# Two 3x3 convolutions read three horizontally shifted copies of their input instead of windows of one padded copy

## The reference, cut to what matters

```python
x_top    = conv1x1(x, w_top);  x_center = conv1x1(x, w_center)     # 16 channels each
x_bottom = conv3x3(x, w_bottom, pad=1)                             # 128 channels
sp_map = einsum('bnp,bpm->bnm', x_center, x_top)                   # 256 x 256 per image
sp_map = softmax(sp_map.reshape(bsz, -1), axis=1)                  # one softmax per image
sp_map = einsum('bnm,bmc->bnc', sp_map, x_bottom)
return conv3x3(x + sp_map.reshape(x.shape), w_out, pad=1)
```

## Time and profile before

| | |
|---|---|
| median of 3 runs | 411.04 us (409.38 to 413.88) |
| the profiled execution | 410.04 us, of which the span in the trace is 408.3 us |
| first convolution, start of its first and last matmul | 14.59 and 31.50 us of the span |
| second convolution, the same | 31.75 and 49.70 us |
| PE busy | 386.3 us, 95% of the span |
| DVE, ACT, POOL busy | 258.3, 282.5, 152.6 us |

### The profile page before, as it was taken

The page is one execution under the profiler, slowest core; times in us unless marked ns, Lnnn a source line. Parts: engine busy times, 40 slices in busy tenths (PEclk is TensorE's granted clock), DMA queues, the critical chain, the costliest instruction groups (busy, mean ns, idle before and its releaser), DMA issues.

```text
span 408.3 us, 5044 instructions
## 1 busy us (share of the span) xinstructions
PE 386.3 (95%) x1641; PEld 273.7 (67%) x1641; DVE 258.3 (63%) x557; ACT 282.5 (69%) x502; POOL 152.6 (37%) x126
## 2 busy tenths in 40 slices
PE   8999989989999889999999999999999999988993
PEld 3588656443646667787787767877777777655782
DVE  0654246884342688566774995766957497777774
ACT  4241235945210967777979989999999998887881
POOL 3810000740085427421458584121232366332253
PEclk9999999999999999999999999999999999999998
DMA  8940000000000023571111004034040002120331
GB/s 263 451 165 0 2 1 0 1 2 0 0 2 0 1 64 109 219 284 53 26 32 46 0 8 125 28 80 177 3 129 26 27 26 79 52 79 0 104 101 56
DMA packets 10674, 28.77 MB, mean 70 GB/s; under 512 B 1079, under 2 KB 2231, under 8 KB 10392
## 3 DMA queue, kind: packets, MB, share of 16 engines
q1 hardware_dynamic: 10648, 28.45, 20.5%
HBM read 27.82 MB, written 0.62 MB: 70 GB/s over the span
## 4 chain that ended last, share of the span: by engine, by line
PE 64%; ACT 17%; DVE 15%; issue 3%; POOLq 0%; POOL 0%; ACTq 0%; DVEq 0%
PE ps L411 16%; PE ps L412 15%; PE ps L413 15%; ACT hidh L966 5%; ACT ps L967 4%; PE ps L418 3%; DVE hidl L1287 2%; PE ps L656 2%; PE ps L423 2%; ACT rstd L875 2%; ACT rstd L877 2%; PE ps L602 1%; DVE bot L1209 1%; DVE small L1208 1%; PE ps L646 1%
## 5 line engine op out<-in xcount | busy, mean ns | idle before, releaser
L1287 DVE TENSOR_TENSOR hidl<-ps,hidh 128x512 fp32r<-128x512 f32 x160 | 108.6, 687 | 52.7 <-ACT ps L967 51.1
L382 POOL TENSOR_TENSOR x<-x,parts 128x512 f32<-128x512 f32 x43 | 55.8, 1298 | 148.1 <-DVE parts L1297 99.7
L411 PE MATMUL ps<-xh,wh_all 128*128 128x512 f32 x160 | 73.0, 456 | 2.2 <-DVE hidl L1287 1.3
L966 ACT ACTIVATE hidh<-ps,par 128x512 fp32r<-128x512 f32 x96 | 68.1, 709 | 8.5 <-PE ps L413 6.8
L411 PE MATMUL ps<-hidh,wh_all 128*128 128x512 f32 (+1 forms) x162 | 64.3, 397 | 4.4 <-DVE hidl L1287 3.8
L967 ACT ACTIVATE ps<-ps,par 128x512 f32<-128x512 f32 x96 | 65.4, 681 | 0.0
L412 PE MATMUL ps<-hidh,wl_all 128*128 128x512 f32 (+1 forms) x162 | 63.5, 392 | 0.0
L412 PE MATMUL ps<-xh,wl_all 128*128 128x512 f32 x160 | 63.5, 397 | 0.0
L413 PE MATMUL ps<-hidl,wh_all 128*128 128x512 f32 (+1 forms) x162 | 63.3, 390 | 0.0
L413 PE MATMUL ps<-xl,wh_all 128*128 128x512 f32 x160 | 63.0, 393 | 0.0
L372 POOL TENSOR_TENSOR wl_all<-wa,wh_all 128x512 fp32r<-128x512 f32 x40 | 50.7, 1283 | 3.5
(11 more groups left out here) (227 smaller groups left out, 569.2 us busy)
## 6 DMA issues: line engine op xcount, KB each, us to landing
scores_all<-rows_scratch SPq DMA_DIRECT2D x48, 256.0 KB, 3.3
wa<-in_moe SPq DMA_DIRECT2D x2, 4096.0 KB, 16.5
wa<-in_moe SPq DMA_DIRECT2D x1, 2048.0 KB, 9.4
dft_x<-in_dft_x SPq DMA_DIRECT2D x1, 640.0 KB
dft_o<-in_dft_o SPq DMA_DIRECT2D x1, 640.0 KB
w<-in_w_bottom SPq DMA_DIRECT2D x1, 576.0 KB, 7.0
w<-in_w_out SPq DMA_DIRECT2D x1, 576.0 KB, 8.8
cst<-in_consts SPq DMA_DIRECT2D x1, 512.5 KB, 7.8
```

The lines of the kernel that those rows point to most:

```text
L382: pool.tensor_tensor(half(x, h), half(x, h), parts[:, n % 2, :], ALU.add).then_inc(s["state_added"], 1)
L411: pe.matmul(o, wh, xhi, start=start, stop=False)
L966: act.activation(hidh[:, n % 2, f, :], sums, func, bias=bias).then_inc(s["hidden_hi_act"], 1)
L1287: dve.tensor_tensor(hidl[:, n % 2, f, :], bank(sums_bank(n, f)), f32(hidh[:, n % 2, f, :]), ALU.subtract).then_inc(s["hidden_lo"], 1)
```

## The change

`xph` and `xpl` are kept three times, once for each horizontal shift `dx`, as [3, 4 images, 18 rows, 16 pixels]: the rows keep their border above and below, and have none left and right, since copy `dx` holds the columns dx to dx+15 of `xp`. A window of a tap is then, per image, 16 rows that follow each other without a gap, 256 elements. The taps run by column: dx = 0 with its three dy first, then dx = 1, then dx = 2. PE waits ahead of each dx for that copy alone. `top` and `cen` move into `wb`, which is free at that time.

```diff
-            xph = sb("xph", [C, B, PAD, PAD], F32R, scope)
-            xpl = sb("xpl", [C, B, PAD, PAD], F32R, scope)
+            xph = sb("xph", [C, 3, B, PAD, SIDE], F32R, scope)
+            xpl = sb("xpl", [C, 3, B, PAD, SIDE], F32R, scope)
...
+        top, cen = wb[:, 0, 0:PIX], wb[:, 0, PIX:2 * PIX]
...
+        def shifted(t, h, dx):
+            return t[:, 2 * h:2 * h + 2, :, dx:dx + SIDE]
...
                 for h in halves:
-                    pe.wait_ge(hi_done, n0 + h + 1)
-                    pe.wait_ge(lo_done, n0 + h + 1)
                     for t in range(9):
                         if (h, t) in between:
                             between[h, t]()
-                        dy, dx = divmod(t, 3)
-                        wh = w33h[:, which, t * C:(t + 1) * C]
-                        wl = w33l[:, which, t * C:(t + 1) * C]
-                        win = (slice(None), slice(2 * h, 2 * h + 2), slice(dy, dy + SIDE), slice(dx, dx + SIDE))
+                        dx, dy = divmod(t, 3)
+                        if dy == 0:
+                            if dx < 2:
+                                pe.wait_ge(early_hi, 2 * h + dx + 1)
+                                pe.wait_ge(early_lo, 2 * h + dx + 1)
+                            else:
+                                pe.wait_ge(hi_done, n0 + h + 1)
+                                pe.wait_ge(lo_done, n0 + h + 1)
+                        w = (3 * dy + dx) * C
+                        wh = w33h[:, which, w:w + C]
+                        wl = w33l[:, which, w:w + C]
+                        win = (slice(None), dx, slice(2 * h, 2 * h + 2), slice(dy, dy + SIDE), slice(None))
...
+            def shift_high(h, dx):
+                act.wait_ge(s["normed"], h + 1)
+                ins = act.activation(xph[:, dx, 2 * h:2 * h + 2], shifted(xp, h, dx), ACT.Copy)
+                ins.then_inc(s["shift_hi" if dx < 2 else "norm_hi"], 1)
+
             for h in range(2):
-                act.wait_ge(s["normed"], h + 1)
-                act.activation(xph[:, 2 * h:2 * h + 2].rearrange("p b y x -> p (b y x)"),
-                               xp[:, 2 * h:2 * h + 2].rearrange("p b y x -> p (b y x)"), ACT.Copy).then_inc(s["norm_hi"], 1)
+                shift_high(0, h)
...
+            shift_high(0, 2)
+            for dx in range(3):
+                shift_high(1, dx)
```

On DVE the low parts of `xp` are six instructions instead of two (`norm_lo` is signalled by the third copy of each half), spread over the list; those of `yp` are six instead of two, in place:

```diff
-            for h in range(2):
-                dve.wait_ge(s["norm_hi"], h + 1)
+
+            def shift_low(h, dx):
                 dve.wait_ge(s["normed"], h + 1)
-                seg = [t[:, 2 * h:2 * h + 2].rearrange("p b y x -> p (b y x)") for t in (xpl, xp, xph)]
-                dve.tensor_tensor(seg[0], seg[1], f32(seg[2]), ALU.subtract).then_inc(s["norm_lo"], 1)
+                if dx < 2:
+                    dve.wait_ge(s["shift_hi"], 2 * h + dx + 1)
+                else:
+                    dve.wait_ge(s["norm_hi"], h + 1)
+                ins = dve.tensor_tensor(xpl[:, dx, 2 * h:2 * h + 2], shifted(xp, h, dx), f32(xph[:, dx, 2 * h:2 * h + 2]), ALU.subtract)
+                ins.then_inc(s["shift_lo" if dx < 2 else "norm_lo"], 1)
+
+            for dx in range(3):
+                shift_low(0, dx)
...
                 dve.tensor_reduce(mx[:, b:b + 1], bank(b), AX.X, ALU.max).then_inc(s["score_max"], 1)
+            shift_low(1, 0)
             dve.wait_ge(s["max_turned"], 1)
...
             dve.tensor_copy(nmx, bank(6, cols=B, first=256)).then_inc(s["neg_max"], 1)
+            shift_low(1, 1)
+            shift_low(1, 2)
             shift_weights(0)
             shift_weights(1)
```

More of the change, by code:

```diff
@@ L84 @@
     "borders_zero", "quiet_zero", "wb_split", "wo_split", "we_split", "pool_step",
-    "centered", "squared", "variance", "log_var", "rstd", "normed", "norm_hi", "norm_lo",
+    "shift_hi", "shift_lo", "mix_shift_hi", "mix_shift_lo", "centered", "squared", "variance", "log_var", "rstd", "normed", "norm_hi", "norm_lo",
     "dve_step",
@@ L142, in metaformer @@
             bot_t = sb("bot_t", [C, TT, C], scope=scope)
-            top = sb("top", [C, PIX], scope=scope)
-            cen = sb("cen", [C, PIX], scope=scope)
             we = sb("we", [C, E * C], scope=scope)
@@ L448, in _, with conv33 @@
                     last.then_inc(s["proj_done"], 1)
-            def conv33(which, hi, lo, hi_done, lo_done, n0, done, halves=(0, 1), between={}):
+            def conv33(which, hi, lo, early_hi, early_lo, hi_done, lo_done, n0, done, halves=(0, 1), between={}):
                 for h in halves:
-                    pe.wait_ge(hi_done, n0 + h + 1)
-                    pe.wait_ge(lo_done, n0 + h + 1)
                     for t in range(9):
@@ L511, in _ @@
             pe.wait_ge(s["wb_split"], 1)
-            conv33(0, xph, xpl, s["norm_hi"], s["norm_lo"], 0, s["bottom_done"],
+            conv33(0, xph, xpl, s["shift_hi"], s["shift_lo"], s["norm_hi"], s["norm_lo"], 0, s["bottom_done"],
                    between={(0, 6): turn_max, (0, 7): spread_max,
@@ L525, in _ @@
             pe.wait_ge(s["wo_split"], 1)
-            conv33(1, xph, xpl, s["mix_hi"], s["mix_lo"], 0, s["out_conv_done"],
+            conv33(1, xph, xpl, s["mix_shift_hi"], s["mix_shift_lo"], s["mix_hi"], s["mix_lo"], 0, s["out_conv_done"],
                    between={(0, 2): lambda: turn_bottom(1), (0, 3): lambda: sum_exp(1), (0, 4): lambda: mix(1),
@@ L917, in mix_high @@
                 act.wait_ge(s["mix_added"], 2 * h + 2)
-                act.activation(xph[:, 2 * h:2 * h + 2].rearrange("p b y x -> p (b y x)"),
-                               yp[:, 2 * h:2 * h + 2].rearrange("p b y x -> p (b y x)"), ACT.Copy).then_inc(s["mix_hi"], 1)
+                for dx in range(3):
+                    ins = act.activation(xph[:, dx, 2 * h:2 * h + 2], shifted(yp, h, dx), ACT.Copy)
+                    ins.then_inc(s["mix_shift_hi" if dx < 2 else "mix_hi"], 1)
             mix_high(0)
@@ L1158, in mix_half @@
                                              rs[:, b:b + 1], inside(xp, b), ALU.mult, ALU.add).then_inc(s["mix_added"], 1)
-                dve.wait_ge(s["mix_hi"], h + 1)
                 dve.wait_ge(s["mix_added"], 2 * h + 2)
-                seg = [t[:, 2 * h:2 * h + 2].rearrange("p b y x -> p (b y x)") for t in (xpl, yp, xph)]
-                dve.tensor_tensor(seg[0], seg[1], f32(seg[2]), ALU.subtract).then_inc(s["mix_lo"], 1)
+                for dx in range(3):
+                    if dx < 2:
+                        dve.wait_ge(s["mix_shift_hi"], 2 * h + dx + 1)
+                    else:
+                        dve.wait_ge(s["mix_hi"], h + 1)
+                    ins = dve.tensor_tensor(xpl[:, dx, 2 * h:2 * h + 2], shifted(yp, h, dx), f32(xph[:, dx, 2 * h:2 * h + 2]), ALU.subtract)
+                    ins.then_inc(s["mix_shift_lo" if dx < 2 else "mix_lo"], 1)
             dve.wait_ge(s["borders_zero"], 2)
```

## The result

The changed kernel takes 414.57 us, median of 20 runs (413.41 to 419.31), where the kernel before takes 411.76 (409.32 to 414.68, 20 runs): a ratio of 1.0099, 95% interval 1.0071 to 1.0126, so about 4.1 us or 1% slower. The two medians lie 2.8 us apart; the executions of either kernel spread over more than 5 us. The profiled execution took 414.10 with a span of 412.3 us, 4.0 longer than the span before.

What follows compares the result with a forecast made beforehand. PE was taken to bound the kernel through both convolutions. Net gain -2.3, idle time +5.6 and clock +1.9 summed to +5.2, making 415.2 or 416.2; the forecast was 415.8 us, range 408.4 to 419.0.

Steps and rivals of the forecast that it cites:

- The gain: Both convolutions on PE: 108 matmuls go from 0.2575 to 0.235 us each, 2.4 us saved, bounds nothing and 2.4.
- 0.1 given back: Ahead of tap 7 of half 0, PE waits longer for DVE's maxima and spread_max, about 0.1 us.
- The copies: ACT and DVE make twelve copies and subtractions instead of four; no tap waits, cost 0, otherwise 0.7 us per half.
- the six: DVE's six shift_weights instructions ahead of the copy to bot_t, forecast to get in one per POOL instruction, ending at 30.0.
- POOL's wait: POOL's weight split waits for norm_lo until 21.9, delaying DVE and bot_t; PE idles 5.6 us before mix(0), bounds 0 to 6.0.
- The clock: Behind PE's idle time before mix(0), clock falls from 2.4 to 1.2 GHz; 1.9 us lost, bounds 0 to 3.
- the clock did fall: Against the rival of the same idle time before mix(0) with the clock staying up: 414.3 or 413.3 us, chance 0.15.
- DVE got one in per end, not two: Against the short-stall rival: two DVE instructions at each POOL end, PE idles 2.3 us, clock holds, 411.0 us; chance 0.13.
- L1157's form collided: Against the faster rival: DVE's shift_weights come through ahead of or beside POOL, bot_t by 25, 408.7 or 407.7 us; chance 0.18.
- the pace did move: Against the rival that conv matmuls stay at 0.2575 us and the stall still comes: 418.4 us, chance 0.07.

Runs made afterwards that it cites:

- the six moved: Changed kernel with shift_weights(0) and (1) moved on DVE from ahead of mix_half(0) to behind the first x1_ready: 407.78 us, ratio 0.9901 to the kernel before.
- the late split: Kernel before, padded layout kept, with POOL's second weight split waiting for neg_max instead of norm_lo at 2: 418.82 us, ratio 1.0164.
- three moved: Changed kernel with only shift_weights(1) moved behind the first x1_ready, shift_weights(0) left in place: 409.68 us, ratio 0.9939 to the kernel before.
- the control: Kernel before, padded layout kept, with shift_weights(0) and (1) moved behind the first x1_ready: 412.81 us, ratio 0.9993.
- POOL later: Changed kernel with POOL's second weight split waiting for bottom_ready at 1 instead of norm_lo at 2: 412.09 us, ratio 1.0002 to the kernel before.
- POOL earlier: Changed kernel with POOL's second weight split waiting for norm_lo at 1 instead of 2: 410.49 us, ratio 0.9976 to the kernel before.
- the matmuls on zeros: Changed kernel with 18 matmuls on zeros put on PE ahead of mix(0): 413.81 us, ratio 1.0051 to the kernel before.

## Why the prediction came out as it did

It was right in sign and mechanism, and near in size: 415.8 was forecast, the median of the runs is 414.57. That the ratio on the later median of 411.76 gives 415.8 too is luck: that median lies 0.7 above the 411.04 that the forecast was built on, and the forecast's sum was 1.2 above the measured one. By its own steps, against the span's +4.0:

- **The gain**, forecast -2.4 and 0.1 given back: 108 x (0.2575 - 0.233) = -2.65; at `spread_max` next to nothing came back. The size holds, the reason was half wrong. I took it for a cost of 32 broken rows against 2. Rows of 20 with dx = 0 are broken and run at 0.240, so breaks alone cost about 0.007 of the 0.0245; a contiguous window off its 16 bytes costs 0.006. That leaves about half of the gain to the two meeting in the rows of 18; no run takes it apart further. That a matmul's time is purely its number of columns is not what these runs show: the same 512 columns took 0.233 to 0.284.
- **The copies**, forecast 0: ACT's take 0.67, DVE's 0.75 (forecast 0.68 and 0.76), and the taps had each in time. Shown by the run with the six moved, which keeps them all and idles nowhere in the convolutions. Two small slips did not matter: ACT's added work is 12 x 0.68 - 4 x 0.745 = 5.2, not 5.4, and the pair of L1127 shows 1.59 - 0.83 = 0.76 from start to start, for 648 columns.
- **POOL's wait**: `norm_lo` was forecast for 21.9 and came at 21.5; the six were forecast to end at 23.3, 26.05, 27.1, 29.65 and 30.0 after the first and ended at 22.84, 25.59, 26.56, 29.05 and 29.43; idle time forecast 5.6, measured 5.24. Shown by the late split in the kernel before, by three and by six moved.
- **The clock**, forecast 1.9: the 16 matmuls of `mix(0)` took 3.57 instead of 1.88, 1.7 us; with the clock kept up 1.4 of it goes, and 0.3 stays (2.15 against 1.88), as it does behind the wait with three moved. The lower level lasted from about 30.0 to 33.4, near the lower end of my 3.2 to 5 us; behind the 5 stood no row. My reading of the earlier trace rows was wrong: I put the fall at about 404.2, 2 us after PE's last matmul, but the window that ends at 406 has the full clock:

```profile
404.00:406.00 2.00, 0.00 (x0) 0.00 (x0) 1.61 (x4) 0.00 (x0) 0.23 (x1) 1.00 0.00 0
```

The 2.0 us at the lower level lie behind it, so the fall came at about 406.2, 4 us after PE stopped. An idle time of 5.6 us was longer than either, so the forecast stood.
- **Not forecast**: the first convolution starts 0.27 earlier (14.39 against 14.66). Without any change of layout it starts at 14.36 in the control's trace, so this is no gain of the change. Sum by these rounded terms: -2.65 + 5.24 + 1.7 - 0.27 = +4.0, which is the measured one. The prediction's sum of +5.2 is 1.2 too high, by small misses in one direction in all its terms.
- **The rivals**: the clock did fall; DVE got one in per end, not two; L1157's form collided, with 128 columns as with 32; and the pace did move.

## What to carry to other kernels

When a semaphore is raised later, list who waits for it on the engines that nobody is looking at: here an unchanged line on POOL moved by 6.5 us into the one stretch where it could hold DVE up. Small DVE instructions from SBUF to SBUF (here tensor_scalar and scalar_tensor_tensor) cost one whole POOL instruction each if POOL is running and they depend on one another; reductions and copies out of PSUM did not wait. Moved to where DVE idles with POOL idle too, the six cost nothing, and a layout that was 1% slower became 1% faster. For a matmul's input, avoid windows whose rows are both broken and off 16 bytes: contiguous (0.239) or on 16 bytes (0.240) was each within 0.007 us of the best.

## What the runs showed of the hardware that was not expected

- A matmul of 512 columns in this float format comes every 0.233 us from contiguous columns, 0.239 when they start 4 bytes off, 0.240 from 32 runs of 16 that start on 16 bytes, 0.2575 with rows of 18, 0.264 with rows of 19 and 22, and 0.284 with rows of 20 that start 4 or 8 bytes off. Why 18 columns are better than 19 and 22 stays open.
- How the granted clock fell isn't told by the length of the idle time alone. In the changed kernel it fell at about 30.0, 5 us after PE had stopped. With POOL later PE idled 2.3 us and was back at work for 1.0 us when the clock fell; with POOL earlier it was 1.5 us and 1.8 us. In the late split and with the matmuls on zeros a wait of 1.1 and 1.0 us at the first tap was followed by 3 us at 0.50 and 0.54, while with three moved, behind 1.4 us of idle time, the clock stayed at 1.00 from 26 to 32 us.

```profile
15.00:18.00 3.00, 3.00 (x8) 2.31 (x8) 2.76 (x5) 0.00 (x0) 0.00 (x0) 0.50 1.01 437
```

- Such dips go with part of the spread of one and the same kernel: with the six moved in the kernel before, five of 12 runs have a mean granted clock of 0.996 or 0.997 and take 409.5 to 410.5 us, the other seven 0.985 to 0.993 and take 412.7 to 414.7. But the kernel before also ran in 409.3 us at 0.991 and in 412.0 at 0.997, and in the changed kernel's trace a dip between 142 and 147 us cost 1.2 us at 149 us and nothing any more at 151. So the clock is not all of the spread, and no run changed the dips by themselves.
